# Dissolving the modulation stage of an adaLN transformer block into the first batch of its attention

## The reference

```python
mod = (_silu(L0_c) @ L0_wmod).reshape(L0_c.shape[0], 6, 1, -1)
sa, ca, ga, sb, cb, gb = (mod[:, 0], mod[:, 1], mod[:, 2], mod[:, 3], mod[:, 4], mod[:, 5])
ga = (2 * (ga >= 0) - 1) * jnp.maximum(jnp.abs(ga), 0.25)
gb = (2 * (gb >= 0) - 1) * jnp.maximum(jnp.abs(gb), 0.25)
h = _layernorm(x, axis=-1) * (1 + ca) + sa
x = x + ga * _L0_attn_ref(h, L0_attn_W_attn, L0_attn_W_proj)
h = _layernorm(x, axis=-1) * (1 + cb) + sb
x = x + gb * _L0_ffn_ref(h, L0_ffn_W1, L0_ffn_b1, L0_ffn_W2, L0_ffn_b2, L0_ffn_W3, L0_ffn_b3)
```

## Time and profile before

| | |
|---|---|
| median of three runs | 1635.27 us (1635.02 to 1635.39) |
| the profiled execution's own time | 1635.03 us |
| its span | 1633.2 us |
| TensorE busy | 1524.7 us, 93% |
| TensorE weight loads busy | 1345.3 us, 82% |
| VectorE busy | 947.4 us, 58% |
| ScalarE busy | 639.6 us, 39% |
| POOL busy | 441.2 us, 27% |

### The profile page before, as it was taken

How to read it: one execution, slowest core, us unless ns; L and a number is a source line. 1 busy time by engine, 2 the same in 40 slices (tenths; PEclk the granted TensorE clock), 3 DMA queues, 4 the chain that set the end, 5 groups by cost and what they waited for, 6 DMA issues and landing times.

```text
span 1633.2 us, 33455 instructions
## 1 busy us (share of the span) xinstructions
PE 1524.7 (93%) x12032; PEld 1345.3 (82%) x12032; DVE 947.4 (58%) x2191; ACT 639.6 (39%) x1282; POOL 441.2 (27%) x456
## 2 busy tenths in 40 slices
PE   5489999999999999984899999999999999999998
PEld 1367878787878787863899999999999999999998
DVE  2467778787778777664744444444544444444442
ACT  2137676766676666682421112211221212121211
POOL 0326565656565656571000000000000000000000
PEclk9599999999999999996899999999999999999999
DMA  5153434353434343415410011101110011000100
GB/s 232 34 140 88 117 94 120 87 122 85 118 90 119 88 115 92 98 49 170 146 46 34 26 33 45 45 0 45 45 45 16 29 45 45 27 31 32 46 14 13
DMA packets 75272, 116.98 MB, mean 72 GB/s; under 512 B 10568, under 2 KB 27976, under 8 KB 74704
## 3 DMA queue, kind: packets, MB, share of 16 engines
q1 hardware_dynamic: 68816, 107.31, 23.9%
q10 hardware_dynamic: 6400, 8.92, 1.5%
HBM read 48.52 MB, written 16.81 MB: 40 GB/s over the span
## 4 chain that ended last, share of the span: by engine, by line
PE 52%; DVE 1%; DMA 1%; SPq 0%; ACT 0%; issue 0%; POOL 0%; DVEq 0%; POOLq 0%
PE feature L1222 33%; PE token L1203 17%; PE feature L1193 1%; PE token L1184 1%; DVE w L1134 1%; DMA b_rows<-b 0%; DMA w_ring<-wproj_t 0%; DVE y L1088 0%; DVE wproj L1134 0%; DVE y L1086 0%; ACT w L1040 0%; DVE attn_tiles L1112 0%; SPq L964 0%; POOL mlp_rstd L1001 0%; DVE gated L1126 0%
## 5 line engine op out<-in xcount | busy, mean ns | idle before, releaser
L1222 PE MATMUL feature<-y,w 128*128 128x256 f32 x3072 | 377.4, 284 | 5.3 <-DVE w L1134 5.3
L1222 PEld LDWEIGHTS feature<-y,w 128*128 128x128 f32 x3072 | 374.1, 190 | 6.9 <-DVE w L1134 5.6
L1034 ACT ACTIVATE mlp_full<-feature,b_cols 128x256 f32<-128x256 f32 x256 | 119.8, 474 | 648.0 <-PE feature L1222 618.0
L485 POOL TENSOR_TENSOR prob_lo<-prob,prob_hi 128x512 f16<-128x512 f32 x256 | 296.5, 1164 | 133.5 <-ACT prob L573 133.1
L1086 DVE CAST y<-mlp_full 128x256 fp32r<-128x256 f32 x256 | 75.1, 293 | 302.3 <-ACT mlp_full L1034 302.0
L566 ACT ACTIVATE prob_hi<-key_score 128x512 f16<-128x512 f32 x320 | 191.0, 597 | 122.6 <-PE key_score L789 119.9
L1001 POOL TENSOR_TENSOR mlp_rstd<-mlp_var_eps,mlp_minus_half 128x2 f32<-128x2 f32 x16 | 11.1, 696 | 798.8 <-DVE mlp_var_eps L1107 798.8
L726 PE MATMUL lin<-h_parts,wqkv 128*128 128x512 f32 x768 | 214.7, 403 | 1.2 <-DVE h_parts L616 1.2
L1222 PEld LDWEIGHTS feature<-turned,w 128*128 128x128 f32 x1536 | 189.2, 191 | 5.1 <-DVE w L1134 3.8
L1222 PE MATMUL feature<-turned,w 128*128 128x256 f32 x1536 | 189.8, 285 | 3.4 <-DVE turned L1088 3.4
L573 ACT ACTIVATE prob<-key_score 128x512 f32<-128x512 f32 x320 | 190.6, 596 | 0.0
(11 more groups left out here) (94 smaller groups left out, 1903.7 us busy)
## 6 DMA issues: line engine op xcount, KB each, us to landing
stack<-qk_parts SPq DMA_DIRECT2D x384, 128.0 KB, 2.4
x_tiles<-x SPq DMA_DIRECT2D x32, 256.0 KB, 3.3
attn_dram<-o_rows SPq DMA_DIRECT2D x32, 256.0 KB, 2.4
attn_tiles<-attn_dram SPq DMA_DIRECT2D x16, 512.0 KB, 4.3
res_tiles<-x SPq DMA_DIRECT2D x16, 512.0 KB, 3.6
out<-res_tiles ACTq DMA_DIRECT2D x16, 512.0 KB, 2.8
wmod_sb<-wmod SPq DMA_DIRECT2D x4, 1536.0 KB, 16.2
w_ring<-w_t SPq DMA_DIRECT2D x12, 512.0 KB, 6.5
```

Source lines behind the costliest of these rows:

```text
L485: nc.gpsimd.tensor_tensor(prob_lo[:, key[1] % 2, u, :], prob[:, u, :], prob_hi[:, key[1] % 2, u, :], ALU.subtract).then_inc(lo_pool, 1)
L1034: nc.scalar.activation(full[:, f % 2, :], fbank[f % 4][:, 0:CH], ACT.Relu, bias=bias[:, f:f + 1])\
L1222: mm = nc.tensor.matmul(fbank[f % 4][:, 0:CH], weights[:, wl, c, f * P:(f + 1) * P], data[:, dl, c, :], start=(c == 0 and i == 0), stop=(c ...
```

## The change

The block of its own for the modulation is gone, and what it did is spread over the start of the attention block.

- Loads: x of batch 0 comes first on SyncE's queue, then the QKV weights in six pieces of 256 columns (all 512 rows each, 1 KB runs), in the order in which q, k and v of the first and the second half of the heads need them. ScalarE's queue carries c and the shift and scale blocks of `wmod` for attention (512 columns each, 2 KB runs). The other two pairs of blocks, shift and scale of the MLP and the two gates, are loaded into the same two buffers from SyncE's queue, each pair after TensorE is done with the one before.
- Shift and scale come as columns: 32 matmuls with the `wmod` block as weights (128x128) and silu(c) as the 8 moving columns, into `o_bank`. Attention's 32 stand first on TensorE, the MLP's behind QK 1. VectorE copies the shifts and adds one to the scales.
- Gates come as rows, 4 matmuls each, in slot 0 at steps 2 and 4, into the key banks; VectorE finishes each in five operations in slot 1 at steps 0 and 2. SyncE writes them in slot 1 at step 3; ScalarE waits for that write at slot 2, since `prob` lies over their memory.
- Weights: ScalarE casts and VectorE subtracts three pieces ahead of the first turn, three behind the last; TensorE waits for the piece it needs.
- POOL sets the ones of v and of the first quarter of the stack ahead of line 453, and those of the three other quarters behind `before_first`. The stack is now four tensors.

```diff
+SHIFT, SCALE, GATE = range(3)
+MOD_LOADS = [(3 * s + j, j) for s in range(2) for j in (SHIFT, SCALE)] + [(3 * s + GATE, s) for s in range(2)]
+W_BLOCK = 2 * P
+W_ORDER = [0, C, 2 * C, W_BLOCK, C + W_BLOCK, 2 * C + W_BLOCK]
...
             load_x(0)
-            for item in before_first():
-                after_item(0, item)
+            for k, first in enumerate(W_ORDER):
+                sp.dma_start(w_block(raw, k), wqkv_t.rearrange("(c p) n -> p c n", p=P)[:, :, first:first + W_BLOCK])\
+                    .then_inc(raw_in[k], 16)
+            for step in (1, 2):
+                sp.wait_ge(mod_mm, step)
+                for half in range(2):
+                    load_mod(sp, 2 * step + half)
+                for item in before_first():
+                    if item[0] == QK and item[1] // 2 == step - 1:
+                        after_item(0, item)
...
+                    if first and (p, u) == (1, 3):
+                        sp.wait_ge(gate_step, GATE_STEPS)
+                        sp.dma_start(gate_dram.rearrange("b (g n) -> b g n", g=2), gates[:]).then_inc(gates_out, 16)
...
+            nc.gpsimd.memset(v[:, :, :, 3 * D:VW], 1.0).then_inc(ones_ready, 1)
+            ones(0)
+            pool.wait_ge(ones_ready, 2)
             inverse_deviation(0)
...
+            pool.wait_ge(h_low, NC_)
+            pool.wait_ge(v_split, V_CREDITS + sum(item[0] == V and last_item(item) for item in before_first()))
+            ones(1)
+            pool.wait_ge(w_lo, len(W_ORDER))
+            for g in range(GROUPS // 2, GROUPS):
+                ones(g)
+            pool.wait_ge(ones_ready, 1 + GROUPS)
...
+            act.dma_start(cc[:], c_t.rearrange("(c p) b -> p c b", p=P)).then_inc(c_in, 16)
+            for i in range(2):
+                load_mod(act, i)
...
+            def weights_high(k):
+                act.wait_ge(raw_in[k], 16)
+                nc.scalar.copy(w_block(wqkv[:, 0], k), w_block(raw, k)).then_inc(w_hi, 1)
...
+                if first and p == 2:
+                    act.wait_ge(gates_out, 16)
...
+            def take_columns(s):
+                dve.wait_ge(mod_mm, s + 1)
+                made = o_bank[:, s * 2 * NC_ * B:(s + 1) * 2 * NC_ * B].rearrange("p (j b) -> p j b", b=B)
+                nc.vector.tensor_copy(mod_cols[:, s, 0:NC_, :], made[:, 0:NC_]).then_inc(mod_taken, 1)
+                nc.vector.tensor_scalar_add(mod_cols[:, s, NC_:2 * NC_, :], made[:, NC_:2 * NC_], 1.0)\
+                    .then_inc(mod_taken, 1)
+
+            def take_gate(g):
+
+                rows = key_bank[g][0:B, :]
+                dve.wait_ge(mod_mm, 3 + g)
+                nc.vector.tensor_scalar(sign[:, g], rows, 0.0, 0.5, ALU.is_ge, ALU.subtract).then_inc(gate_step, 1)
+                nc.vector.tensor_copy(gates[:, g], rows).then_inc(gate_step, 1)
+                dve.wait_ge(gate_step, 5 * g + 2)
+                nc.vector.scalar_tensor_tensor(out=gates[:, g], in0=gates[:, g], scalar=-1.0, in1=gates[:, g],
+                                               op0=ALU.mult, op1=ALU.max).then_inc(gate_step, 1)
+                dve.wait_ge(gate_step, 5 * g + 3)
+                nc.vector.tensor_scalar(gates[:, g], gates[:, g], GATE_FLOOR, 2.0, ALU.max, ALU.mult)\
+                    .then_inc(gate_step, 1)
+                dve.wait_ge(gate_step, 5 * g + 4)
+                nc.vector.tensor_tensor(gates[:, g], gates[:, g], sign[:, g], ALU.mult).then_inc(gate_step, 1)
...
             row_stats(0, range(NT))
             variance(0)
             normalise(0, range(NT))
+            for k in range(3):
+                weights_low(k)
+            take_columns(0)
+            dve.wait_ge(mod_taken, 2)
+            take_mod(0)
             for item in before_first():
                 after_item(0, item)
+                if item == (TURN, NC_ - 1):
+                    for k in range(3, len(W_ORDER)):
+                        weights_low(k)
+            take_columns(1)
...
+                    if first and p == 1 and u in (0, 2):
+                        take_gate(u // 2)
...
+            def mod_columns(s):
+                for j in (SHIFT, SCALE):
+                    pe.wait_ge(wm_in[j], 16 * (s + 1))
+                    for block in range(NC_):
+                        at = ((s * 2 + j) * NC_ + block) * B
+                        for c in range(NC_):
+                            mm = nc.tensor.matmul(o_bank[:, at:at + B], wm[:, j, c, block * P:(block + 1) * P],
+                                                  silu[:, c, :], start=(c == 0), stop=(c == NC_ - 1))
+                mm.then_inc(mod_mm, 1)
+
+            def gate_rows(g):
+                pe.wait_ge(wm_in[g], 16 * 3)
+                for c in range(NC_):
+                    mm = nc.tensor.matmul(key_bank[g][0:B, :], silu[:, c, :], wm[:, g, c, :],
+                                          start=(c == 0), stop=(c == NC_ - 1))
+                mm.then_inc(mod_mm, 1)
+
             pe.sem_inc(pv_done, PV_CREDITS)
+            pe.wait_ge(silu_step, 3)
+            mod_columns(0)
+            pe.wait_ge(pool_step, 8)
             for item in before_first():
                 do_item(0, item)
-            pe.wait_ge(ones_ready, 2)
+                if item == (QK, 1, NC_ - 1):
+                    pe.wait_ge(mod_taken, MOD_STEPS)
+                    mod_columns(1)
...
             def slot(b, p, first, more):
+                if first and p == 2:
+                    pe.wait_ge(gate_step, GATE_STEPS)
+                    pe.wait_ge(ones_ready, 1 + GROUPS)
+                if first and p == 3:
+                    pe.wait_ge(mod_taken, 2 * MOD_STEPS)
                 for u in range(UNITS):
+                    if first and p == 0 and u in (2, 4):
+                        gate_rows(u // 2 - 1)
```

More of the change, by code:

```diff
@@ L312, in attention @@
     qk_parts = mem.sb("qk_parts", [P, 2, 2, 2, T], F32R)
-    stack = mem.sb("stack", [P, 2, H, T], F32R)
+    stack = [mem.sb(f"stack{g}", [P, 2, 4, T], F32R) for g in range(GROUPS // 2)]
+    with ExitStack() as raw_ctx:
+        raw = Memory(nc, raw_ctx).sb("wqkv_raw", [P, NC_, 3 * C])
+    stack += [mem.sb(f"stack{g}", [P, 2, 4, T], F32R) for g in range(GROUPS // 2, GROUPS)]
     v = mem.sb("v_parts", [P, NT, H, VW], BF16)
@@ L317, in attention @@
     max_rows = mem.sb("max_rows", [2 * NT, 2, P], F32R)
+    with ExitStack() as gate_ctx:
+        gmem = Memory(nc, gate_ctx)
+        sign = gmem.sb("gate_sign", [B, 2, C])
+        gates = gmem.sb("gates", [B, 2, C])
     prob = mem.sb("prob", [P, UNITS, 512])
+    with ExitStack() as wm_ctx:
+        wm = Memory(nc, wm_ctx).sb("wmod_sb", [P, 2, NC_, C])
     prob_hi = mem.sb("prob_hi", [P, 2, UNITS, 512], F16)
@@ L347, in lin_no, with w_block, w_ready, load_mod @@
         return LIN * n + ORDER.index(unit)
+    def w_block(tile, k):
+        return tile[:, :, W_ORDER[k]:W_ORDER[k] + W_BLOCK]
+    def w_ready(f):
+        at = (f % 2) * C + f // 2 * P
+        return 1 + max(k for k, first in enumerate(W_ORDER) if first <= at < first + W_BLOCK)
+    def load_mod(engine, i):
+        column, half = MOD_LOADS[i]
+        engine.dma_start(wm[:, half], wmod.rearrange("(c p) n -> p c n", p=P)[:, :, column * C:(column + 1) * C])\
+            .then_inc(wm_in[half], 16)
     def lin_bank_of(unit):
@@ L410, in load_stack @@
                         step = 2 + k_part - q_part
-                        sp.dma_start(f32(stack[32 * block_row:32 * block_row + 32, :, 4 * g + j, :]),
+                        sp.dma_start(f32(stack[g][32 * block_row:32 * block_row + 32, :, j, :]),
                                      src[:, q_part:q_part + step + 1:step, :]).then_inc(stack_in[g], 16)
@@ L776, in scores_by_query @@
                     head, n = 2 * p + hh, P * (t + 1)
-                    mm = nc.tensor.matmul(bank[:, col:col + n], stack[0:3 * D, 0, head, t * P:(t + 1) * P],
-                                          stack[0:3 * D, 1, head, 0:n], start=False, stop=True,
+                    rows = stack[head // 4][0:3 * D, :, head % 4, :]
+                    mm = nc.tensor.matmul(bank[:, col:col + n], rows[:, 0, t * P:(t + 1) * P], rows[:, 1, 0:n],
+                                          start=False, stop=True,
                                           skip_group_check=True)
@@ L788, in scores_by_key @@
                     head, n = 2 * p + hh, T - P * t
-                    mm = nc.tensor.matmul(bank[:, col:col + n], stack[0:3 * D + 2, 1, head, t * P:(t + 1) * P],
-                                          stack[0:3 * D + 2, 0, head, t * P:T], start=False, stop=True,
+                    rows = stack[head // 4][0:3 * D + 2, :, head % 4, :]
+                    mm = nc.tensor.matmul(bank[:, col:col + n], rows[:, 1, t * P:(t + 1) * P], rows[:, 0, t * P:T],
+                                          start=False, stop=True,
                                           skip_group_check=True)
```

174 lines of the change are left out of this document (56 added, 118 removed).

## The result

The kernel after takes **1648.9 us** (median of four runs, 1647.1 to 1650.2) where the kernel before takes 1635.3 (four runs, 1635.0 to 1636.2): 1.0084 times the time before, 95% interval 1.0068 to 1.0100. I had forecast 1602.3. The profiled execution took 1647.1, its span is 1645.3.

The account below looks back on a forecast made before the run. TensorE was taken as the bound nearly everywhere, with a serial chain before its first dense work; -42.4 (earlier scores) - 1.2 + 6.9 + 4.0 = -32.7 from 1635.03 gave 1602.3 us, range 1594 to 1612.

Parts of the forecast that it names:

- Steady state: The work after the first slots: same instructions as before, so 0 us of change.
- slots past 2 last longer than before: Named sign that the prediction is wrong: attention slots after slot 2 taking longer than in the kernel before.
- a clock that stays low (D): Rival: half clock persists through batch 0's attention, adding 70 us, 1672 us; chance 0.02.
- First QKV matmul, 24.0: Start: loads, normalisations and first column set let the first QKV matmul begin at 24.0 us instead of 69.09.
- 150 ns: Named sign that the prediction is wrong: column weight loads over 150 ns apart; 110 ns was expected at full clock.
- rival B: Thin column matmuls keep the half clock: first QKV matmul near 28 (+4), second set +3, 1609.3 us; chance 0.20.
- Second set, 7.0: MLP's shift and scale columns on TensorE's path behind QK 1: 7.0 us, scores 22.0 us after the first QKV matmul.
- A's 64 ns: Rival of cheap columns: pairs at 64 ns (-2.9), gate work absorbed by VectorE's slack (-4.0), 1594.4 us; chance 0.17.
- No stack wait: Before the scores: stack loads arrive in time, so TensorE's former 4.03 us wait for them is gone.
- Gate rows, +6.9: Slot 0, steps 2 and 4: 2 x 8 records at 0.43 us, all on TensorE, +6.9 us.
- clock's -1.2: V matmuls before the scores: without the idle stack wait the clock does not drop, -1.2 us.
- take_gate, +4.0: VectorE's gate operations in slot 1: 6.3 us for two halves, bounds 0 and 6.3, taken as +4.0 us.

Follow-up runs that it names:

- e3: Kernel after with 80 waits on a value long reached (40 instructions) at the start of TensorE's stream: 1664.5 us, one run.
- e1: Kernel after with 164 do-nothing waits (82 instructions) at the start of TensorE's stream, moving its loop on: 1616.2 us, 0.9875 of the kernel before.
- e2: Kernel before with 344 do-nothing waits (172 instructions) ahead of line 203's matmuls, moving its loop on: 1676.7 us, 1.0246.
- e7: Kernel after without the second set of columns (MLP's shift and scale left out), no waits added: 1610.8 us, 0.9850 of the kernel before.
- e8: Kernel after without the gates (ones in their place), no waits added: 1608.7 us, 0.9843 of the kernel before.
- e6: e5 with 41 bf16 identity matmuls ahead of the first set, in place of the waits: 1610.1 us, 0.9845 of the kernel before.
- e9: e6 with x of batch 1 asked for behind stack 0, ahead of the gate loads and stack 1: 1612.9 us, 0.9851 of the kernel before.
- e10: e9 with VectorE's gate work of the first half moved to slot 0 step 3, the second to slot 1 step 0: 1608.1 us, 0.9832.
- e5: e1 with the second set of columns spread in eight groups of four matmuls among QK 2 and 3: 1613.6 us, 0.9877 of the kernel before.

## Why the prediction was wrong

By the prediction's own sum the span would have been 1602.3 - 1.8 = 1600.5. It was 1645.3, 44.8 more, and by the stretches of the timeline: +9.9 until the scores (55.9 for 46.0), +2.3 in slots 0 to 7 (89.0 us for 77.0 - 1.2 + 6.9 + 4.0 = 86.7), **+35.3 in the loop**, -2.7 behind it. The last lies within what this stretch differs by between the kernels run here (974.7 to 980.9, e3 apart); I give it no cause.

**Steady state: "same instructions, 0". This step failed**, and with it the sign. The instructions were the same; where they stand was not. e1 and e2 show it from both sides: 33 us back by moving the loop on, 42 lost in the span by moving the loop of the kernel before (35.1 in the rounds, 7.5 ahead of them, of which 4.2 are the waits' own). The prediction had named the sign of it ("slots past 2 last longer than before") but no mechanism, and no rival had one. The chance of 0.02 for slower was given to another one, a clock that stays low (D), which didn't come: in the kernel after it was at half from 75.4 to 89.1, in slots 1 and 2, and full from there to the first return. What the kernel before could have told: its instruction queue has packets all through straight code and none in rounds 2 to 6 of the loop, so the loop was held loaded; the change adds instructions ahead of it.

**First QKV matmul, 24.0: was 28.65.** Mis-sized is the first set, 13.79 us where 9.8 was forecast (8.7 to 18.5). It ran at 0.215 us a pair to its end, where I had assumed the rise of line 203 after 5 us; that is also past the 150 ns which the prediction had named as a sign of being wrong. That is rival B with its price (+4). The half rate is read from the spacing: the second set has the same behind 41.3, where the clock's row shows 0.50. The trace records no change of the clock before 34.5, and the row reads 1.00 all through that time, also while TensorE stands still. VectorE's end (18.6 for 18.3), the normalisations (1.92 for 2.2) and the loads (set begins at 9.1 for 8.7) were right. The Trainium skill (SBUF — State Buffer, "SBUF: two separate sides") has the lock between POOL and VectorE. The trace agrees: with no memset beside them no normalisation was slow.

**Second set, 7.0: was 9.69**, again by B's mechanism, and 2.5 us more in QK 2 at the half clock; scores started 27.2 us behind the first QKV matmul, not 22.0. At full rate the price per pair was right: the 5.35 us from the fall at 41.3 hold 25 pairs at 0.215, which leaves 39 for the 4.34 us before it, 0.11 each. A's 64 ns falls. No stack wait: right, and e7 shows that without the set it comes back with 4.13 us.

**Gate rows, +6.9: 7.2** (two times 3.60). With the clock's -1.2 that makes slot 0, 13.4 us for 13.3.

**take_gate, +4.0: mis-sized.** Slots 1 and 2 took 25.2 us, where the kernel before has 19.0: +6.3. The five operations took 3.1 us (0.67, 0.67, 0.68, 0.41, 0.68), 6.2 for two, as worked out. But without any gate the two slots are +5.0 already (e8), and the gates add 1.1 to that (e1). What the sum lacked is x of batch 1. I had it landing "when VectorE reaches its statistics"; it stood behind 24 stack issues and came 2.4 us late in the kernel after, 5.2 in e6, where the scores begin 9.9 us earlier, and 6.6 in e8, where no gate row holds VectorE back. From e6 to e9 the early x takes 2.9 us off the two slots, from e9 to e10 the moved gate work 3.3. How the 2.3 us by which the kernel after missed the forecast here split between the two is not shown.

With the loop's place put right (e1) the time is 1616.2, still past my range's upper end of 1612: rival B had the half clock right, with 2.9 us too little (7.0 for 9.9), and nothing had the late x.

## What to carry over

Before a change ahead of a long loop, read the page's instruction queue and count the loop: if its packets pause in the loop, the code is held, and the number of instructions ahead decides whether it stays so. When a loop of unchanged work gets slower by the same amount every round, shift it by some do-nothing instructions before anything else is suspected. Thin work spread among dense matmuls left the clock full here, where in one piece it fell. A transfer freed at the start should be followed to whatever else stands in its queue. And when an experiment takes a wait away and the time stays, look slot by slot before the theory is dropped: in e9 the gain was there and another slot had lost it.

## What the runs showed of the chip

- TensorE's code: a loop of 1606 instructions is kept over its rounds at some places within blocks of 256 and loaded again in every round at others. The price is 3.3 us of standing at each return on average and, with the clock at half behind it, 7.1 us a round; the MLP's loop lost 2 to 3 us at each of five returns (e3: 989.2 us behind the attention loop, the others 974.7 to 980.9).
- A wait on a value long reached costs TensorE 0.11 us: 172 such instructions held it until 19.69, 256 until 28.99.
- In the first set, 64 pairs with 8 moving columns in 13.8 us, the spacing stayed at that of the half clock throughout, and in the second set and in e6 the full clock fell within such a run, at 41.3 and 14.6. Eight pairs at a time between QK matmuls left it full (e5, 34 to 50).
